# Down products as one 512-column matmul into both halves of a PSUM bank, in a two-layer MoE and attention kernel

## The reference

```python
def ffn(x):                                   # 4096 tokens of 256
    attn_out = layer_norm(x) * nw + nb
    combine, dispatch = top1_gate(attn_out, wg, capacity=512)       # 8 experts
    dispatched = einsum('sec,sm->ecm', dispatch, attn_out)
    h = gelu(einsum('ecm,emi->eci', dispatched, inter_w) + inter_b)  # 256 -> 1024
    expert_out = einsum('eci,eim->ecm', h, output_w) + output_b      # 1024 -> 256
    moe_out = einsum('sec,ecm->sm', combine, expert_out)
    rh = gelu(attn_out @ res_inter_w + res_inter_b)
    res = rh @ res_output_w + res_output_b
    coef = softmax(attn_out @ res_coef)
    return res * coef[:, :1] + moe_out * coef[:, 1:] + x
```

## Time and profile before

| | |
|---|---|
| median of three runs | 1354.74 us |
| lowest and highest | 1353.83 and 1358.02 us |
| the profiled execution's own time | 1362.24 us |
| its span | 1360.5 us |
| mean granted clock of TensorE | 0.949 |
| busy: TensorE matmul (PE) | 1226.1 us, 90% |
| busy: TensorE weight load (PEld) | 916.0 us, 67% |
| busy: VectorE (DVE) | 919.6 us, 68% |
| busy: ScalarE (ACT) | 711.7 us, 52% |
| busy: GpSimd (POOL) | 308.5 us, 23% |
| first ffn layer, attention, second ffn layer | to about 443, to about 912, to the end (us of the span) |

### The profile page before, as it was taken

One profiled execution on the slowest core, in us unless ns is written; L12 is line 12 of the kernel. 1 busy time (PEld: TensorE's weight loads), 2 busy tenths in 40 slices (PEclk: granted clock), 3 DMA queues, 4 the chain that ended last, 5 costly groups with the idle time before them and its releaser, 6 DMA issues. The chain is left out here.

```text
span 1360.5 us, 29269 instructions
## 1 busy us (share of the span) xinstructions
PE 1226.1 (90%) x11173; PEld 916.0 (67%) x11173; DVE 919.6 (68%) x2031; ACT 711.7 (52%) x1032; POOL 308.5 (23%) x283
## 2 busy tenths in 40 slices
PE   5999949999999269999999999979999689999994
PEld 4999838999999134443444443438998469999984
DVE  5776605788886366787786867576775236888782
ACT  4555414445454036777776778755555134544541
POOL 2120450012121101122221222231220700223233
PEclk8999959999999579999999999998999789999997
DMA  9502120234441362340332303015103311455632
GB/s 269 171 1 70 52 74 16 77 123 144 137 147 47 95 120 35 52 79 18 43 62 40 64 3 63 2 41 136 47 16 93 118 47 62 110 146 139 151 84 28
DMA packets 143915, 109.45 MB, mean 80 GB/s; under 512 B 73084, under 2 KB 131784, under 8 KB 143816
## 3 DMA queue, kind: packets, MB, share of 16 engines
q1 hardware_dynamic: 134600, 91.22, 25.6%
q0 software_dynamic: 9216, 16.85, 5.5%
HBM read 57.06 MB, written 34.21 MB: 67 GB/s over the span
## 5 line engine op out<-in xcount | busy, mean ns | idle before, releaser
L243 ACT ACTIVATE f_h<-f_up,vecT 128x512 f32<-128x512 f32 x256 | 177.0, 691 | 410.2 <-PE f_up L232 319.9
L1337 ACT ACTIVATE a_probs<-a_S 128x1024 f32<-128x1024 f32 (+3 forms) x320 | 272.9, 901 | 78.1 <-PE a_S L1236 41.0
L253 DVE TENSOR_TENSOR f_h_lo<-f_h,f_h_hi 128x512 fp32r<-128x512 f32 x256 | 176.2, 691 | 180.3 <-ACT f_h_hi L243 151.8
L1232 PE MATMUL a_S<-a_QT,a_KT 128*32 128x512 f16 (+3 forms) x2560 | 173.4, 353 | 14.4 <-DMA a_QT<-a_Qf 7.9
L243 ACT ACTIVATE f_h_hi<-f_up,vecT 128x512 fp32r<-128x512 f32 x256 | 174.9, 683 | 0.0
L264 PE MATMUL f_down<-f_w_hi,f_h_hi 128*128 128x256 f32 x512 | 148.5, 290 | 13.3 <-issue 9.1
L1232 PEld LDWEIGHTS a_S<-a_QT,a_KT 128*32 128x32 f16 x2560 | 59.8, 96 | 145.9 <-ACT a_probs L1337 75.9
L265 PE MATMUL f_down<-f_w_lo,f_h_hi 128*128 128x256 f32 x512 | 147.7, 289 | 11.0 <-issue 10.9
L266 PE MATMUL f_down<-f_w_hi,f_h_lo 128*128 128x256 f32 x512 | 148.3, 290 | 8.9 <-issue 8.9
L1510 DVE TENSOR_TENSOR a_probs<-a_probs 128x1536 f32<-128x1536 f32 (+1 forms) x60 | 126.2, 2103 | 39.9 <-ACT a_probs L1337 39.1
L1253 PE MATMUL a_cx<-a_probs,a_V 128*32 128x512 f32 (+3 forms) x1280 | 145.5, 530 | 0.6 <-ACT a_probs L1337 0.6
(11 more groups left out here) (182 smaller groups left out, 2330.3 us busy)
## 6 DMA issues: line engine op xcount, KB each, us to landing
f_aT_all<-in_L_ffn_inter_w SPq DMA_DIRECT2D x32, 512.0 KB, 4.4
f_aT_all<-in_L_ffn_output_w SPq DMA_DIRECT2D x32, 512.0 KB, 5.4
slots_in<-f_zeros SPq DMA_DIRECT2D x16, 516.0 KB, 12.3
f_aT_all<-slots_in SPq DMA_DIRECT2D x16, 516.0 KB, 4.8
out<-x_all SPq DMA_DIRECT2D x9, 512.0 KB
x_all<-in_L_attn_x SPq DMA_DIRECT2D x8, 512.0 KB, 9.2
moe_rows<-f_zeros SPq DMA_DIRECT2D x8, 512.0 KB, 8.0
a_moe<-moe_rows SPq DMA_DIRECT2D x6, 512.0 KB, 4.0
```

Of the source, the lines that this page charges most:

```text
L243: i = self.nc.scalar.activation(to, self.up_ps[k % UP_BANKS][:], ACT.Gelu_apprx_tanh, bias=bias)
L253: nc.vector.tensor_tensor(lo, h, hi, ALU.subtract).then_inc(self.h_split, 1)
L1232: last = nc.tensor.matmul(S[hp][k:k + DH, i, lo:CH], KT[:, h, j * P + k:j * P + k + DH], QT[:, c % 2, h, lo:CH], start=True, stop=not diag)
L1337: nc.scalar.activation(probs[:, q % P_RING, hp * 2:hp * 2 + 2, lo:CH], S[hp][:, :, lo:CH], ACT.Exp).then_inc(exp_done[hp], 1)
```

## The change

The high and the low part of w2 (and of ew2) now lie side by side in SBUF, 256 and 256 columns. For each tile of a down group, h_hi meets both parts in one matmul of 512 columns that fills the whole bank: its first half collects h_hi x w2_hi, its second h_hi x w2_lo. h_lo x w2_hi goes to the first half as before. So a group has 8 matmuls and 8 weight loads instead of 12 and 12, with the same number of columns. When the chunk is done VectorE first adds the bias to the first halves as before, raises a new semaphore `half_read`, waits for it, and adds the second halves with four more additions, each of which raises `evacuated`; TensorE waits for it bank by bank instead of once.

```diff
     def down(self, pe, c, k, w2_hi, w2_both, first):
         nc = self.nc
         pe.wait_ge(self.h_split, c * NK + (k + 1))
-        if k == 0 and not first:
-            pe.wait_ge(self.evacuated, c)
         for t in range(TT):
+            if k == 0 and not first:
+                pe.wait_ge(self.evacuated, (c - 1) * TT + (t + 1))
             hi = self.h_hi[:, k % HS_RING, t * P:(t + 1) * P]
             lo = self.h_lo[:, k % HS_RING, t * P:(t + 1) * P]
-            bank = self.down_ps[t][:, 0:D]
-            nc.tensor.matmul(bank, hi, w2_hi, start=(k == 0), stop=False)
-            nc.tensor.matmul(bank, hi, w2_lo, start=False, stop=False)
-            last = nc.tensor.matmul(bank, lo, w2_hi, start=False, stop=(k == NK - 1))
+            nc.tensor.matmul(self.down_ps[t][:], hi, w2_both, start=(k == 0), stop=False)
+            last = nc.tensor.matmul(self.down_ps[t][:, 0:D], lo, w2_hi, start=False, stop=(k == NK - 1))
         last.then_inc(self.down_done, 1)
...
-        ew2 = [sb(f"ew2_{n}", [P, W_RING, D], F32R) for n in ("hi", "lo")]
+        ew2_both = sb("ew2", [P, W_RING, 2, D], F32R)
+        ew2 = [ew2_both[:, :, n, :] for n in range(2)]
...
-        w2 = [sb(f"w2_{n}", [P, NK, D], F32R) for n in ("hi", "lo")]
+        w2_both = sb("w2", [P, NK, 2, D], F32R)
+        w2 = [w2_both[:, :, n, :] for n in range(2)]
...
-                    sp.wait_ge(m.evacuated, NC + (e - 1))
+                    sp.wait_ge(m.evacuated, (NC + (e - 1)) * TT)
...
                 for t in range(TT):
                     i = v.tensor_tensor(part[:, t, :], m.down_ps[t][:, 0:D], eb2[:, parity, :], ALU.add)
-                i.then_inc(m.evacuated, 1)
-                dve.wait_ge(m.evacuated, c + 1)
+                i.then_inc(s["half_read"], 1)
+                dve.wait_ge(s["half_read"], c + 1)
+                for t in range(TT):
+                    v.tensor_tensor(part[:, t, :], m.down_ps[t][:, D:2 * D], part[:, t, :], ALU.add).then_inc(m.evacuated, 1)
+                dve.wait_ge(m.evacuated, c * TT + TT)
                 for t in range(TT):
                     i = v.tensor_scalar(part[:, t, :], part[:, t, :], weight_now[:, t:t + 1], None, ALU.mult)
```

More of the change, by code:

```diff
@@ L253, in split_h, with down @@
         nc.vector.tensor_tensor(lo, h, hi, ALU.subtract).then_inc(self.h_split, 1)
-    def down(self, pe, c, k, w2_hi, w2_lo, first):
+    def down(self, pe, c, k, w2_hi, w2_both, first):
         nc = self.nc
         pe.wait_ge(self.h_split, c * NK + (k + 1))
-        if k == 0 and not first:
-            pe.wait_ge(self.evacuated, c)
         for t in range(TT):
+            if k == 0 and not first:
+                pe.wait_ge(self.evacuated, (c - 1) * TT + (t + 1))
             hi = self.h_hi[:, k % HS_RING, t * P:(t + 1) * P]
             lo = self.h_lo[:, k % HS_RING, t * P:(t + 1) * P]
-            bank = self.down_ps[t][:, 0:D]
-            nc.tensor.matmul(bank, hi, w2_hi, start=(k == 0), stop=False)
-            nc.tensor.matmul(bank, hi, w2_lo, start=False, stop=False)
-            last = nc.tensor.matmul(bank, lo, w2_hi, start=False, stop=(k == NK - 1))
+            nc.tensor.matmul(self.down_ps[t][:], hi, w2_both, start=(k == 0), stop=False)
+            last = nc.tensor.matmul(self.down_ps[t][:, 0:D], lo, w2_hi, start=False, stop=(k == NK - 1))
         last.then_inc(self.down_done, 1)
@@ L279, in tensor_chunk @@
                 k = s - AHEAD
-                _, _, w2_hi, w2_lo = weights(pe, k, False)
-                self.down(pe, c, k, w2_hi, w2_lo, first)
+                _, _, w2_hi, w2_both = weights(pe, k, False)
+                self.down(pe, c, k, w2_hi, w2_both, first)
                 if beside and k in beside:
@@ L388, in ffn_block @@
         scatter_at = sb("scatter_at", [P, NT], U32)
-        s = split_sems(ctx, nc, tag, "stat_chain var_ready rstd_ready y_ready y_kept turned aT_all_ready aT_ready lin_ready "
+        s = split_sems(ctx, nc, tag, "stat_chain var_ready rstd_ready y_ready y_kept turned half_read aT_all_ready aT_ready lin_ready "
                        "logits_done logits_read dif_ready th_ready updated gate lm_ready ex_ready hot_ready "
@@ L399, in ffn_block @@
         cols = [slice(0, INTER // 2), slice(INTER // 2, INTER)]
-        pieces = [([w[:, :, cols[0]] for w in w1], mem["w1_first"][:]), ([w[:] for w in w2], raw2),
+        pieces = [([w[:, :, cols[0]] for w in w1], mem["w1_first"][:]), (w2, raw2),
                   ([w[:, :, cols[1]] for w in w1], raw1[:, :, cols[1]])]
@@ L865, in weights @@
                 n = slice(k * P, (k + 1) * P)
-                return (lambda kd: w1[0][:, kd, n]), (lambda kd: w1[1][:, kd, n]), w2[0][:, k, :], w2[1][:, k, :]
+                return (lambda kd: w1[0][:, kd, n]), (lambda kd: w1[1][:, kd, n]), w2[0][:, k, :], w2_both[:, k].rearrange("p a d -> p (a d)")
             def norms(c):
@@ L898, in weights @@
                         pe.wait_ge(s["e_split"], e * NK + (k + 1))
[L899 removed]
+                    return (lambda kd: ew1[0][:, r, kd, :]), (lambda kd: ew1[1][:, r, kd, :]), ew2[0][:, r, :], ew2_both[:, r].rearrange("p a d -> p (a d)")
                 m.tensor_chunk(pe, e + NC, weights, False, None if last else {EARLY: lambda: turn_slots(e + 1)})
```

## The result

The changed kernel takes 1401.84 us (median of four runs, 1400.23 to 1405.77) against 1354.74 us: 1.0344 times as long, 95% interval 1.0319 to 1.0369, so 47.1 us slower. The forecast was +18.0 us, and 1383 us as the upper end of its range. The direction was right, the size was not: 29 us are missing. The profiled execution takes 1400.23 us with a span of 1398.5 us, 38.0 us more than the profiled one of before, which was 7.5 us over its median; this one is the fastest of its four. Two executions are left out of the ratios of the experiments, one of e5 with 4241.89 us (the median given for e5 counts it; without it that is 1351.49) and one of the kernel before beside it with 2480.56 us; what held them is not known.

The account below looks back on a forecast made before the run. TensorE was taken to set the pace in the chunk stages, VectorE having 4 us to spare in 25. Terms -5.9 + 5.9 + 5.0 + 3.0 + 9.6 + 2.9 - 2.5 = +18.0 us gave 1372.8 us, range 1362 to 1383.

Parts of the forecast that it names:

- the fourth point of part 3: Second-layer experts: VectorE, GpSimd's stores and landing form a closed loop; each turn lengthens by 1.45 us, +9.6 us in all.
- part 2: Four more PSUM additions per chunk cost VectorE 1.45 us; TensorE's wait on `evacuated` and SyncE's moved bias load cost nothing.
- Matmuls, -5.9: Where TensorE sets the pace, one start saved per token tile gives 8.9 ns, 0.285 us per chunk, -5.9 us in all.
- Rival 1: Weight loads bound TensorE's pace, so a tile saves 38.3 ns: sum -1.5 us, 1353.2 us, no change; 8%.
- Additions, 1.45 us: VectorE's extra time before each scaling or update, stalling TensorE at joints: token chunks +5.9 and +5.0 us.
- The stall into chunk 5: TensorE's stall of 1.0 us between token chunks 4 and 5, taken as lost in the slow stretch that follows.
- First-layer experts, 23.3 to 23.8: Forecast us per first-layer expert with the additions; stalls at their joints sum to +3.0 us.
- The sum of these with a closed loop at constant landing: Plain terms without the creep term: -5.9 + 5.9 + 5.0 + 3.0 + 9.6 + 2.9 = +20.5 us.
- Rival 3: Second-layer loop isn't closed: stores land while VectorE works anyway, experts cost as in the first layer; 1364.3 us, 6%.
- Rival 4: The 512-column matmuls run as two pieces and save no start: matmul term 0, 1378.7 us; 8%.
- Rival 2: Creep, TensorE's slow starts in chunk 5 during GpSimd's scatter, goes: 1332.3 us both layers, 1353.8 one; 4% each.
- The term of -2.5 us: Chunk 5, both layers: TensorE's slow matmuls during the scatter each carry more work, 0.84 group pairs more by its end.

Follow-up runs that it names:

- e5: Changed kernel with the factor folded into the additions (eight VectorE operations per chunk) and second-layer weight load behind the stores: 1352.38 us, 0.9969 of before.
- e1: Changed kernel, but in the second layer SyncE waits for the previous expert's stores before loading the next expert's second weight half: 1369.44 us, 1.0081 of before.
- e3: Changed kernel without the four second additions and their semaphore, so the output lacks h_hi x w2_lo: 1301.64 us, 0.9585 of before.
- e7: Changed kernel with the second additions left out in the experts alone, token chunks keeping them: 1357.32 us, 1.0001 of before.
- e8: Kernel before, with token chunks 5 and 6 written out instead of looped over: 1357.91 us, 1.0010 of before.
- e4: Kernel before, with a memset of about 1.45 us on GpSimd ahead of each second-layer expert's four stores: 1377.87 us, 1.0153 of before.
- e6: Changed kernel with the second additions left out in the token chunks alone, experts keeping them: 1378.05 us, 1.0156 of before.
- e15: Changed kernel with GpSimd waiting after each eighth scatter to land, and the second-layer weight load issued behind the stores: 1322.69 us, 0.9760 of before.
- e13: Kernel before, with GpSimd waiting for its scatters to have landed after each eighth, nothing else: 1305.18 us, 0.9634 of before.
- e9: e5 with GpSimd's 32 scatters per layer in four groups of eight, later groups waiting for TensorE's down groups: 1298.56 us, 0.9562 of before.
- e12: e5 with GpSimd waiting for its scatters to have landed after each eighth, then going on at once: 1298.55 us, 0.9559 of before.

## Why the prediction was wrong

**The step that failed** is the fourth point of part 3, the experts of the second layer: "Additions, scaling, GpSimd's stores, their landing and four splits form a closed loop of 23.48 us in which TensorE has no part; 1.45 us lengthen each turn by 1.45." The loop is there and closed, but its landing was taken as a constant 2.6 us. A load was issued with the end of the last store's issue, off another chain: SyncE waits for VectorE's weight split at k = 3. The step named no transfer beside the stores, and part 2 looked at SyncE only for the bias load ("Both cost nothing"). Landing took 5.1 to 6.1 us in the six turns, and a turn 29.2 us. Laid side by side, one turn of the changed kernel (GpSimd's start to the next, 1213.72 to 1243.98) is 30.26 us against 23.48:

| part of a turn | before | after | e1 |
|---|---|---|---|
| GpSimd's start to its last store's end | 8.16 | 8.61 | 8.78 |
| landing | 2.60 | 5.93 | 2.33 |
| release of VectorE to GpSimd's next start | 12.72 | 15.72 | 14.16 |

From GpSimd's start the load comes after 1236.60 - 1228.51 = 8.09 us before, and after 7.34 us now, since VectorE's spare time between the splits takes up 0.75 of the 1.45 us; the stores take 0.45 us longer. Together the load gains 1.2 us on the last store. (The two chains aren't free of each other. In every turn of before, e3, e7 and e8 that end lies 0.06 to 0.07 us behind the load's issue, though GpSimd's way to it varies from 8.05 to 8.6 us. What ties them is not shown.) The third row has the 1.45 us of additions in both kernels with them; the 1.56 us by which after exceeds e1 stand beside TensorE's stop of 4.31 us and its restart at 1.2 GHz. So TensorE has a part in the turn after all, once VectorE is late enough. Over six turns, 29.2 - 24.9 makes 26 of the missing 29 us; the other 3 are spread over terms that no run tells apart. e1 takes the 26 back and e4 makes them in part without any new addition, and the queues show the load's packets on the DMA engines while the stores land. So this cause is shown; by what rule an engine takes packets from the two queues is only inferred.

**The rest, step by step.**
- *Matmuls, -5.9.* The pitches were as forecast; first-layer experts without additions take 23.1 us (23.4 before). The sum has a slip: by its own 0.036 and 0.285 us, chunks 5 to 7 save 0.71 us a layer and not 0.67. Rival 1, a pace set by weight loads, fell: PEld went from 22.90 to 20.91 of 25 us and a tile still takes 0.34 to 0.35 us.
- *Additions, 1.45 us.* Right. At the token joints h_lo(0) is followed by down(0) within 0.05 to 0.14 us, in chunks 1 to 3 h_lo(2), in chunk 4 h_lo(1). e6 bears them out joint by joint. The stall into chunk 5 was put at nothing, and in both layers down(0) of chunk 5 came 1.2 us later behind that of chunk 4 than before (with the matmuls' saving taken off).
- *First-layer experts, 23.3 to 23.8.* 23.35 measured.
- *The sum of these with a closed loop at constant landing.* e15 against e13: 17.5 us, about 23 once the creep left in e13 is set aside, against 20.5 us and the 2.4 into chunk 5. The forecast described a kernel whose loads stay out of the way.
- *Rival 3* (the loop isn't closed) fell: e1's turns are 1.5 us longer than before.
- *Rival 4* (no start saved) fell by the pitches.
- *Rival 2* (the creep goes) didn't happen in this change. The term of -2.5 us isn't shown: its 0.84 group pairs have no working in the prediction, and the runs can't tell it from nothing. But it was no idle rival: the same TensorE program, with or without a few VectorE instructions, has it (after), has part of it (e6) or loses most of it (e3). Its price of 21.5 us a layer was too low: from chunk 5 to 7 the kernel before takes 73.6 and 73.0 us against 45.6, so it is worth some 28. (For one layer alone the rival's time should be 1372.8 + 1.25 - 21.5 = 1352.6, since half of the term stays.)
- *The range.* Its upper end came from more VectorE time at 30 places. No bound stood for "VectorE's delay makes two transfers meet", though in the trace the load's issue (1236.60) and the last store's end (1236.67) lay 0.07 us apart.

## What to carry to other kernels

A delay on a side engine isn't spent where it is counted: before it is priced at its own length, look which transfers it moves and which it leaves, and how far apart in the trace the two are issued. If it is less than the delay, order them by a wait. In this kernel it was also worth 51 us to break up a long run of indirect DMAs, on an engine that TensorE doesn't wait for; elsewhere that has to be tried.

## What the runs showed of the hardware

A store of GpSimd whose issue ends 0.5 us behind that of a 1 MB load lands in 4.7 us instead of 2.3 (e4, e1), and while it does, the DMA engines move both queues' packets. During 32 scatters without a pause other engines start their instructions late with nothing to wait for, from some 19 us behind the first until a few microseconds behind the last (before, first layer: its issue ends at 193.14, the DMA engines move nothing from 195 on, and ScalarE starts again at 197.30). In the kernel before it is TensorE and beside it ScalarE, with a gap of 22.61 us; in the changed kernel it is above all ScalarE, whose gelu starts behind a gap of 20.53 us, and TensorE waits for it:

```profile
177.66 0.68 ACT L243 ACTIVATE f_h_hi<-f_up,vecT 128x512 fp32r<-128x512 f32 x1
198.87 0.69 ACT L243 ACTIVATE f_h<-f_up,vecT 128x512 f32<-128x512 f32 x1 [20.53 <-remote]
...
200.59 0.70 ACT L243 ACTIVATE f_h_hi<-f_up,vecT 128x512 fp32r<-128x512 f32 x1
```

The up product that it reads, up(4), was issued by 171.31 and all else that it waits for (h_lo(2), down(0)) was done by then too. What holds the engines up stays open: from 165 to 200 us the trace of before has the scatters' packets alone, none of an instruction queue and none of a load, and no semaphore, and writing out the loop (e8) changed nothing. A fetch that is asked for and held back wouldn't show, so it isn't ruled out. That it needs scatters in a row is shown by e9, e12 and e13; why e3 nearly escapes it with 32 in a row is open too.
